# Four-layer graph network on one core: deeper rings in layer 1, all late counts moved into layer 0

## The reference

```
x = x + L0(h): mean over in-edges of h[src], concatenated with h, times W, plus b
x = x + L1(h): theta = h[dst] - h[src]; w = sigmoid(relu(theta @ W1 + b1) @ W2 + b2)
               segment_sum(w * theta, dst) + indegree * (h @ W4 + b4)
x = x + L2(h): g = relu(h @ Wp.T + bp); mean of g[src] over in-edges; linear; elu; row-normalised; plus h
x = x + L3(h): segment_sum(all_h[type, src] * edge_weight, dst) + h @ loop_weight
```

## Time and profile before

| what | value |
|---|---|
| median of three runs | 6216.14 us (6207.88 to 6224.03) |
| profiled execution | 6220.82 us, span 6218.9 us |
| stretch of layer 0's sums | 108 to 1120 us |
| stretch of layer 1's edges | 1197 to 3480 us |
| stretch of layer 2's sums | 3545 to 4130 us |
| stretch of layer 3's edges | 4344 to 6219 us |
| busy over the span | PE 62%, DVE 46%, ACT 23%, POOL 60% |

### The profile page before, as it was taken

The page is one execution under the profiler, slowest core; times in us unless marked ns, Lnnn a source line. Parts: engine busy times, 40 slices in busy tenths (PEclk is TensorE's granted clock), DMA queues, the critical chain, the costliest instruction groups (busy, mean ns, idle before and its releaser), DMA issues.

```text
span 6218.9 us, 69225 instructions
## 1 busy us (share of the span) xinstructions
PE 3862.1 (62%) x20719; PEld 2994.6 (48%) x20719; DVE 2875.8 (46%) x9736; ACT 1423.7 (23%) x5476; POOL 3717.9 (60%) x3922
## 2 busy tenths in 40 slices
PE   4888888665555555555555488867466655665433
PEld 3445555554444444455555366644344444454332
DVE  7776666555444555555555533343332222222222
ACT  5333333332222233333333301122000000000000
POOL 4234444266666666666666466645666666666665
PEclk7799999777767777777777799988777777777666
DMA  3233333444444444444444455545111111111121
GB/s 108 83 112 117 127 136 136 128 138 135 141 136 135 140 140 137 146 140 139 139 147 142 135 189 202 200 158 188 45 46 46 46 46 46 47 45 47 46 63 48
DMA packets 310271, 707.07 MB, mean 114 GB/s; under 512 B 72640, under 2 KB 155292, under 8 KB 297612
## 3 DMA queue, kind: packets, MB, share of 16 engines
q0 software_dynamic: 159184, 377.89, 21.5%
q1 hardware_dynamic: 148700, 323.81, 15.0%
q10 hardware_dynamic: 2016, 0.92, 0.1%
HBM read 571.29 MB, written 131.05 MB: 113 GB/s over the span
## 4 chain that ended last, share of the span: by engine, by line
PE 32%; another core or an unknown queue 28%; DVE 21%; issue 15%; ACT 3%; DVEq 1%; SPq 1%; DMA 0%; POOL 0%; ACTq 0%
PE ps L2577 11%; DVE oneh L1866 7%; PE ps L2533 4%; PE ps L2562 3%; DVE ps L2001 3%; PE ps L2472 2%; PE ps L2484 2%; PE ps L2600 2%; PE ps L2540 2%; DVE third L1993 2%; DVE turned_words L1958 2%; DVE tmp L1957 1%; PE ps L2422 1%; PE ps L2536 1%
## 5 line engine op out<-in xcount | busy, mean ns | idle before, releaser
L1473 POOL DMA_INDIRECT rows<-tab_rel,third x1299 | 1250.3, 963 | 626.4 <-issue 369.4
L1473 POOL DMA_INDIRECT rows<-tab_hp,idx_src x1120 | 1084.2, 968 | 556.5 <-issue 307.7
L1473 POOL DMA_INDIRECT rows<-tab_h,idx_src x810 | 779.3, 962 | 857.5 <-PE ps L2540 517.1
L2600 PE MATMUL ps<-third 128*128 128x128 f32 x3126 | 612.1, 356 | 676.5 <-issue 383.5
L2577 PE MATMUL ps<-third,h 128*120 128x385 bf16 (+20 forms) x4606 | 866.4, 335 | 55.4 <-DMA h<-cnt_d 23.0
L2600 PEld LDWEIGHTS ps<-third 128*128 128x128 f32 x3126 | 546.1, 261 | 731.2 <-issue 421.7
L2533 PE MATMUL ps<-oneh,rows 128*128 128x128 f32 x2598 | 476.6, 336 | 565.0 <-issue 297.2
L2533 PEld LDWEIGHTS ps<-oneh,rows 128*128 128x128 f32 x2598 | 426.3, 243 | 640.3 <-issue 342.3
L1684 ACT ACTIVATE turned_words<-turned_words 128x128 f32<-128x128 f32 x1563 | 462.9, 297 | 1101.6 <-DVE turned_words L2006 857.8
L2577 PEld LDWEIGHTS ps<-third,h 128*120 128x120 bf16 (+10 forms) x4606 | 587.3, 131 | 265.5 <-issue 40.6
L1473 POOL DMA_INDIRECT third<-tab_hp,idx_src x443 | 428.4, 967 | 217.6 <-issue 122.4
(11 more groups left out here) (279 smaller groups left out, 4920.3 us busy)
## 6 DMA issues: line engine op xcount, KB each, us to landing
third<-dst_flat SPq DMA_DIRECT2D x390, 256.0 KB
h<-cnt_d SPq DMA_DIRECT2D x48, 1568.0 KB
cnt_d<-h SPq DMA_DIRECT2D x46, 1568.0 KB
tab_rel<-third SPq DMA_DIRECT2D x49, 512.0 KB
rows<-tab_rel,third POOLq DMA_INDIRECT x1299
rows<-tab_hp,idx_src POOLq DMA_INDIRECT x1120
rows<-tab_h,idx_src POOLq DMA_INDIRECT x810
third<-tab_hp,idx_src POOLq DMA_INDIRECT x443
```

Source lines behind the costliest of these rows:

```text
L1473: pool.indirect_dma_start(out=to[:, t, 0:n], out_offset=None, in_=table[:, :], in_offset=bass.IndirectOffsetOnAxis(ap=idx[:, col:col + 1], ...
L2600: last = pe.matmul(ps_t[sl][:, t * P:(t + 1) * P], onehT[:, sl, t * P:(t + 1) * P], pwin[:, st["v"] % 2, :], start=True, stop=True)
```

## The change

It makes the rings of layer 1 deeper, puts more turns between its steps, and drops the late counts:

- slots of gathered rows 7 to 9, the two new ones in space that the late counts and `turned_words` had;
- banks of expansions 2 to 4, `hid`, `zed` and `gate` 2 to 4, transposed one-hots 2 to 4, gated one-hots 3 to 5, windows of target rows 2 to 3; `hid` moves to `tmp_words`;
- banks of sums 2 to 3; the copy of a window out of its bank is planned two turns later, its addition one turn later; two `gsum` buffers instead of one (in layers 0 and 2 too);
- `hidden` and `gates` stand 3 turns behind the gather instead of 2, `onehot` 4 instead of 3 and ahead of `scatter` in the same turn;
- the early transposes of layer 1 share the one bank of the node work instead of having bank 4;
- all 48 bundles are counted and multiplied in layer 0, which gathers from group 292 on instead of 287.

```diff
-HP_SLOT = 7
+HP_SLOT = 9
+NONE1, NBC, NOT, NPW, NHID = 5, 3, 4, 3, 4
+LATE_OUT1, LATE_ADD1 = 2, 2
-        ps_t = ps[0:2]
-        turn_banks = [ps[0], ps[1], ps[4]]
-        far_banks = ps[6:8]
+        ps_t = ps[0:4]
+        turn_banks = [ps[0], ps[1], ps[5]]
+        far_banks = [ps[6], ps[7], ps[4]]
...
-            g0 = (npg0, 0, npg, HEAD_END)[layer]
+            g0 = (npg, 0, npg, HEAD_END)[layer]
...
-                banks = 3 if layer == 3 else 2
+                banks = 3 if layer in (1, 3) else 2
...
             def finish_far(v, scat):
-                st = dict(..., free=n_gturn.get(v - 1, 0))
+                for _ in range(LATE_OUT1 if layer == 1 else 0):
+                    yield
+                st = dict(..., bank=v % (3 if layer == 1 else 2), free=n_gturn.get(v - 2, 0))
...
-                yield
-                plan.append(("far_add", dict(v=v, sums=sums, turn=n_gturn[v], add=s_add.value)))
+                for _ in range(LATE_ADD1 if layer == 1 else 1):
+                    yield
+                plan.append(("far_add", dict(v=v, bank=st["bank"], sums=sums, turn=n_gturn[v], add=s_add.value)))
...
-                plan.append(("onehot_t", dict(g=g, bc=n_bc[g], expand=n_expand.get(g - 2, 0))))
+                plan.append(("onehot_t", dict(g=g, bc=n_bc[g], expand=n_expand.get(g - NOT, 0))))
-                plan.append(("expand", dict(g=g, v=v, oneT=n_oneT[g], pw=n_pw[v], hid=n_hid.get(g - 2, 0))))
+                plan.append(("expand", dict(g=g, v=v, oneT=n_oneT[g], pw=n_pw[v], hid=n_hid.get(g - NHID, 0))))
...
-                steps = ((1, expand), (4, scatter), (2, hidden), (2, gates), (0, gather), (0, fetch_window), (3, onehot),
+                steps = ((1, expand), (4, onehot), (4, scatter), (3, hidden), (3, gates), (0, gather), (0, fetch_window),
                          (0, onehot_t))
-            pack_steps = (plan_packs(0, npt0, NQS), plan_packs(npt0, npt, 2), plan_reload(), plan_dense3())[layer]
+            pack_steps = (plan_packs(0, npt, NQS), iter(()), plan_reload(), plan_dense3())[layer]
```

More of the change, by code:

```diff
@@ L331, in gnn_program @@
         s_add = sem("s_add")
-        s_bc = [sem(f"s_bc{i}") for i in range(3)]
-        s_pw = [sem(f"s_pw{i}") for i in range(2)]
+        s_bc = [sem(f"s_bc{i}") for i in range(NBC)]
+        s_pw = [sem(f"s_pw{i}") for i in range(NPW)]
         s_oneT = sem("s_oneT")
@@ L464, in plan_turn @@
             tr, hT = s_tr.up(), s_hT.up()
-            plan.append(("turn", dict(c=c, m=m, slot=slot, h=h_at[c], pst=pst_free.get(slot, 0), tr=tr,
+            free = None
+            if slot == EARLY:
+                k, free = take_bank()
+                assert node_banks[k] is turn_banks[slot]
+                give_bank(k, s_hT, hT)
+            plan.append(("turn", dict(c=c, m=m, slot=slot, h=h_at[c], free=free, pst=pst_free.get(slot, 0), tr=tr,
                                       hT_free=hT_free.get(slot, 0), hT=hT)))
@@ L847, in scatter @@
                         pass
-                plan.append(("scatter", dict(layer=layer, g=g, v=v, slot=g % slots, sums=sums, one=n_one[g], row=n_row[g],
+                plan.append(("scatter", dict(layer=layer, g=g, v=v, slot=g % slots, bank=v % banks, sums=sums, one=n_one[g], row=n_row[g],
                                              first=first, last=last, add=n_gadd.get(v - banks, added_before if layer == 3 else 0))))
@@ L911, in count @@
                     per_bank = 512 // w
[L912 to L913 removed]
+                    first_bank = k % 4 if nb <= per_bank else 2 * (k % 2)
+                    st = dict(i=i, w=w, start=start, stop=stop, pair=n_pair[i], parts=[])
                     for b, q0 in enumerate(range(0, nb, per_bank)):
@@ L943, in plan_packs @@
                         cost = nb * width_of[k] / 2.4 + next(running, 0.0)
-                        if not late and (i - lag) % PACK == PACK - 1 and k == bundles[bundle_of[k]][-1]:
+                        if (i - lag) % PACK == PACK - 1 and k == bundles[bundle_of[k]][-1]:
                             for more in running:
@@ L1114, in plan_edges @@
                 running[:] = [chain for chain in running if next(chain, "end") != "end"]
-                if layer == 1 and turn == NONE:
-                    plan.append(("iota_late", dict(node=s_node.value, iota=s_iota_late.up())))
                 if layer == 0 and turn == 1:
@@ L1122, in plan_edges @@
                     plan.append((KEYS3_TURNS[turn], keys3))
-                if layer != 1 or turn > NONE:
-                    credit += per_turn
+                credit += per_turn
                 while credit > 0:
@@ L1630, in scalar_program @@
                     if st["store"]:
-                        act.wait_ge(s_cst[st["stored"]].handle, st["store"])
-                    to = counts_late if st["late"] else counts[:, slot, :, :]
+                        act.wait_ge(s_cst[slot].handle, st["store"])
+                    to = counts[:, slot, :, :]
                     for bank, q0, q1, _, _, done in st["parts"]:
@@ L1666, in scalar_program @@
                     at = 0 if st["layer"] == 1 else 2 * P
-                    act.copy(gsum[:, 0:n_part], far_banks[st["v"] % 2][:, at:at + n_part]).then_inc(s_glo.handle, 1)
+                    act.copy(gsum_at[st["v"] % 2][:, 0:n_part], far_banks[st["bank"]][:, at:at + n_part]).then_inc(s_glo.handle, 1)
                 elif kind == "heads_begin":
@@ L1927, in vector_program @@
                 elif kind == "far_out" and st["layer"] != 1:
-                    bank = far_banks[st["v"] % 2]
+                    bank, gsum = far_banks[st["bank"]], gsum_at[st["v"] % 2]
                     dve.wait_ge(s_glo.handle, st["lo"])
```

147 lines of the change are left out of this document (61 added, 86 removed).

## The result

The changed kernel took 6256.7 us (median of 4 runs, 6251.3 to 6260.5), the kernel before 6215.5 us beside it (4 runs, 6207.9 to 6224.0). The ratio is 1.0060, 95% interval 1.0047 to 1.0072: slower, by about 37 us (the medians lie 41 us apart). The profiled execution took 6260.5 us with a span of 6258.7 us, 39.8 us more than before. The forecast was 6169 us; the result lies above the range.

What follows compares the result with a forecast made beforehand. Layer 1 was taken as bound by POOL's gathers plus waits for slots freed late, layer 0 by PE. 6220.8 + 18 - 65 = 6173.8 us, or 6169 us against the runs; range 6072 to 6226, the forecast's own 6110 to 6197.

Steps and rivals of the forecast that it cites:

- Layer 0, +18 us: Layer 0: counting and multiplying all bundles there makes it 18 us longer, with 8 and 28 us as bounds.
- Layer 1, -65 us: Layer 1 as a whole: 46 us saved at layer 3's rate of waiting and some 20 for the late window copy.
- so DVE can work through one more group while a release is late: Layer 1: expansions consumed two turns after PE's turn instead of one; deeper rings priced at -46 us.
- The rate scaled from layer 3: POOL in layer 1: waiting per gather falls from 0.209 to layer 3's 0.179 us, over 1563 gathers -46 us.
- POOL's waits, about 110 and not shorter each: Layer 1's gathers: POOL waits for a slot around 110 times instead of 156, each wait as long as before.
- L2001's waits down by a third: DVE's subtraction in layer 1: its waits for PE, 775 us in all, fall by a third or more.
- So I cost it at nothing: Layer 1's scatter waiting for a one-hot of the same turn: costs nothing; without cover 1.11 us in each turn.
- L1667 and L1943 nearly without waits: Layer 1's window copy and addition: the later turns cover most of ACT's 185.8 us and DVE's 116.9 us.
- The 20 us charged for these waits: Layer 1: some 20 us gained by the late window copy and the late counts' removal, within the -65.
- The slower one: Rival, chance 0.14: in layer 1 longer gather runs make each release later; at 130 waits 6272 us.
- N x 2.44 us: Slower rival's price: N waits of POOL in layer 1 change it by 2.44 N - 279; slower overall from N = 107.

Runs made afterwards that it cites:

- the first comparison: The full changed kernel against the kernel before, both unedited, in the late condition: 6256.7 us against 6215.5 us, ratio 1.0060.
- late: Condition of some comparisons, unedited kernels included, in which TensorE's releases are held up; the kernel before took 6215 to 6285 us.
- prompt: Condition of the other comparisons, in which TensorE's releases come at once; the kernel before, unedited, took 5545 to 5552 us.
- the three late traces with the old rings: The kernel before (6215.5 us); it with only the late counts moved to layer 0 (1.0032); it with only the one-hots ahead of the scatter (1.0013).
- the two with the deep ones: The changed kernel (1.0060 to the kernel before), and the changed kernel with the subtraction put back ahead of the one-hots (1.0045).
- the thinned kernel before: The kernel before, with layer 1 gathering only one of a group's four tiles once the slots are filled: 5179.1 us, ratio 0.833.

## Why the prediction was wrong

- **Layer 0, +18 us: right.** 19.8 us in the first comparison; 0.0032 x 6285 = 20 us for this part alone when late; 0.0038 x 5552 = 21 us for it when prompt, and layer 1's first gather 22.5 us later in the changed kernel's prompt trace. L2577's matmuls (now L2559) rose from 4606 to 4704, the 98 predicted. Taking the counts out of layer 1 gave nothing back, also as said.
- **Layer 1, -65 us: wrong; it measured +12.** The step that failed is "so DVE can work through one more group while a release is late". With the old order kept, the deeper rings left VectorE's wait for TensorE at 667.3 us (before 702.3) and POOL's at 343.7 us (before 326.0). The prediction priced the rings as though a release were late by some fixed time that one more turn can cover. What the runs showed in its place is lateness that grew with the rings: the expansions' releases, as far as they are on record (over nine in ten), came at a median of 5.7 to 5.8 us behind the start of the last matmul in the three late traces with the old rings and 8.0 us in the two with the deep ones, and TensorE itself stood 461 us (old order) instead of 130 between matmuls that wait for nothing. These two figures are worked out from the trace's semaphore records and say that the lateness grew, not why. Why it stands there is open. The rate scaled from layer 3 (0.179 us of waiting per gather) was not an effect of its ten slots that layer 1 could take over: layer 1 has 0.211 with nine. Where releases are prompt, rings had nothing to give at all.
- **POOL's waits, about 110 and not shorter each: 141**, 2.34 us each instead of 2.09, and their sum the same (329.5 us against 326.0).
- **L2001's waits down by a third: down by two thirds, and worth nothing.** The time went into the gates' wait, by the order and not by the rings; with the order undone it came back.
- **"So I cost it at nothing", the one-hots of the same turn:** I looked at TensorE, which waits for them, and not at what they wait for themselves. VectorE's wait for the gates is the price: 508 us of waits in the trace, 485 us of time where neither gathers nor late releases cover it, 8 us in the old rings when late (1.0013), and less than the shorter gathers gave back when prompt (0.9987). The answer, a small cost, was nearly right for the full kernel by luck; the reason was wrong.
- **L1667 and L1943 nearly without waits: half.** ScalarE's copy (now L1660) waits 11.1 us instead of 185.8; VectorE's addition (now L1932) still waits 51.9 us instead of 116.9. The 20 us charged for these waits did not show, as layer 1 gained nothing in all; no late run tells this part from the rest.
- **The rivals.** The slower one had the right sign and the right thought that releases come later, but the wrong place: it wanted longer waits of POOL, N x 2.44 us; POOL's waiting in sum is unchanged. The loss beyond layer 0 (1.0060 against 1.0032, some 17 us, from two different comparisons) lies behind layer 1's last gather (21.5 us more, against 9.5 us saved before it) and at the end of layer 3. That this end took 26.2 us instead of 13.5 is not shown to be due to the change: the other late traces have 19 to 26 us, the 26 in the thinned kernel before, whose layer 3 is the old one.

The rule of the Trainium skill that the prediction weighed (SBUF — State Buffer, "SBUF: two separate sides") says that at SBUF's ports compute and DMA can't slow each other. The prompt traces agree with it: beside 1563 gathers VectorE's L2001 waits 14.9 us in all for TensorE. In the late ones the thinned kernel shows that the gathers take part, but no run shows that it is by a port. Another page of the Trainium skill (Perfetto Trace Analysis, "Tensor Engine Instruction") says that TensorE's end in a profile is modelled, and its release is sent only when PSUM has acknowledged the write. So for a single late release these traces can't tell whether the matmul or its release was held up; TensorE's standing between matmuls, told above, is seen from the starts of the matmuls.

What stays open: by what path the gathers (or the recording of them) hold up TensorE and its releases, why it stands more with deeper rings, what makes the late condition, and why a stop comes every ten gathers whatever the slack is.

## What to carry to other kernels

Before pricing a ring, ask what makes the lateness and what ends it, not only how long it is: here the lateness grew with the rings, and the groups in flight made the stage's end 14 us longer (26.9 against 12.7 us). Look also for time in which an engine stands although its next instruction waits for nothing; a table of waits by line doesn't set it apart. When steps are reordered, ask for each moved step what it waits for as well as who waits for it; thinning the engine that hides the chain shows its own pace in one run.

## What the runs showed of the hardware that I had not expected

The same kernel took 5545 to 5552 us or 6215 to 6285 us, 12 to 13% apart, on one chip at different times too. Layer 1's gathers themselves last 0.96 to 0.97 us in both. Between the two traces of the kernel before, 293 us of the 673 lie in layer 1, 222 in layer 3 and 144 in layer 2, wherever gathers run densely, and 15 before layer 1.

In the late condition TensorE stood up to 2.7 us between two matmuls of one step, the second of which waits for nothing; in no prompt trace did it stand there at all.

TensorE's granted clock followed the order of the steps: with thinned gathers it was 0.95 over layer 1 in the two kernels in which TensorE was idle for 0.8 us of a turn, and 0.83 and 0.84 in the two in which it was idle for 1.4 and 1.6 us (stretch less busy time, over 391 turns). Those means lie between the levels of 1.2 and 2.4 GHz. The same matmuls took 1159 us of TensorE's time instead of 908.
